# Counting edges with one-hots: eight of a kind in one comparison, item innermost

## What is computed

```python
x = _layernorm(x + layer(x, edge_index), axis=-1)
```

```python
agg = jax.ops.segment_sum(x[src], dst, num_segments=n)   # = counts @ x
```

## Time and profile before

| | us |
|---|---|
| median of three runs | 3100.99 |
| lowest, highest | 3099.07, 3108.09 |
| profiled execution | 3096.49 |
| its span | 3094.6 |
| counting stage within it, about | 128 to 562 |

### The profile page before, as it was taken

One profiled execution on the slowest core, in us unless ns is written; L12 is line 12 of the kernel. 1 busy time (PEld: TensorE's weight loads), 2 busy tenths in 40 slices (PEclk: granted clock), 3 DMA queues, 4 the chain that ended last, 5 costly groups with the idle time before them and its releaser, 6 DMA issues. The chain is left out here.

```text
span 3094.6 us, 39006 instructions
## 1 busy us (share of the span) xinstructions
PE 1888.4 (61%) x7042; PEld 1007.8 (33%) x7043; DVE 2296.7 (74%) x4650; ACT 1832.1 (59%) x2352; POOL 1044.7 (34%) x984
## 2 busy tenths in 40 slices
PE   3354555359798567548846666666666666650636
PEld 1122222223333222112233434343433344430636
DVE  4799999479999678768926777777777777775444
ACT  0166666338888444358927877777777777860010
POOL 1000000000000011013207777777777777753000
PEclk8689898555656699869957777777777777765868
DMA  2144444104544499425614555555555555551616
GB/s 84 41 148 147 147 143 143 59 32 164 185 172 177 196 364 373 191 90 209 231 30 146 168 165 166 162 171 166 166 156 170 164 167 161 166 147 29 265 56 223
DMA packets 288619, 490.59 MB, mean 159 GB/s; under 512 B 39166, under 2 KB 237646, under 8 KB 275718
## 3 DMA queue, kind: packets, MB, share of 16 engines
q1 hardware_dynamic: 254694, 394.56, 36.7%
q0 software_dynamic: 26688, 54.65, 7.4%
q10 hardware_dynamic: 7200, 40.96, 3.4%
HBM read 282.58 MB, written 209.91 MB: 159 GB/s over the span
## 5 line engine op out<-in xcount | busy, mean ns | idle before, releaser
L1794 POOL DMA_INDIRECT es_got<-w,es_idx x808 | 882.3, 1092 | 346.1 <-issue 342.4
L1929 PE MATMUL en_pv<-en_sq,avg 128*128 128x512 f32 x202 | 197.7, 1079 | 371.6 <-ACT en_sq L2036 371.6
L1391 PE MATMUL acc<-src_hot,dst_hot 128*128 128x401 f16 x1008 | 231.6, 382 | 186.7 <-DVE src_hot L1366 166.7
L1366 DVE TENSOR_SCALAR src_hot<-iota,col_key 128x400 f16<-128x400 f16 x1008 | 315.9, 313 | 0.0
L1364 DVE TENSOR_SCALAR dst_hot<-iota_blk,row_key 128x128 f16<-128x128 f16 x1008 | 247.4, 245 | 11.9 <-PE acc L1391 11.4
L803 PE MATMUL pd_dn<-hT,pd_lhs 66*128 66x512 f32 (+1 forms) x350 | 233.3, 845 | 23.0 <-DVE pd_top L906 18.2
L2064 ACT COPY es_rows<-es_rp 128x512 f32<-128x512 f32 x202 | 118.2, 585 | 171.7 <-PE es_rp L1911 170.4
L1992 DVE TENSOR_TENSOR es_lg<-es_dn,es_w2p 128x512 f32<-128x512 f32 x101 | 69.5, 688 | 198.1 <-PE es_w2p L1885 198.1
L1391 PEld LDWEIGHTS acc<-src_hot,dst_hot 128*128 128x128 f16 x1008 | 107.2, 106 | 311.4 <-issue 270.8
L1059 PE MATMUL ns_acc<-ns_w,ns_val 128*65 128x512 f32 (+1 forms) x350 | 156.2, 595 | 71.2 <-DVE ns_w L1019 71.2
L1420 ACT COPY cbuf<-acc 128x401 f32<-128x401 f32 x200 | 98.4, 492 | 146.7 <-PE acc L1391 112.8
(11 more groups left out here) (500 smaller groups left out, 4753.9 us busy)
## 6 DMA issues: line engine op xcount, KB each, us to landing
rows<-es_rows SPq DMA_DIRECT2D x202, 256.0 KB, 2.8
counts_part<-cbuf SPq DMA_DIRECT2D x50, 800.0 KB, 3.7
near<-pd_out SPq DMA_DIRECT2D x25, 1600.0 KB, 6.2
ns_near<-near SPq DMA_DIRECT2D x25, 1600.0 KB, 9.8
ns_cnt<-counts_part SPq DMA_DIRECT2D x25, 1600.0 KB, 6.7
ss_cnt<-counts_part SPq DMA_DIRECT2D x25, 1600.0 KB, 6.6
n_ct<-turned ACTq DMA_DIRECT2D x50, 800.0 KB, 6.0
top_plane<-es_mx SPq DMA_DIRECT2D x101, 256.0 KB
```

The source lines that it names most:

```text
L1366: TS(src_hot[:, s, i, 0:PART].unsqueeze(1), k["iota16"][:, 0:PART].unsqueeze(1), k["col_key"][:, bass.ds(BATCH * b + i, 1)], None, ALU.is_ ...
L1391: last = nc.tensor.matmul(flat[:, bass.ds(places[i], PART + 1)], dst_hot[:, s, i, :], src_hot[:, s, i, 0:PART + 1], start=False, stop=Fals ...
L1794: pool.indirect_dma_start(got[:, s, t, half * 2 * F:(half + 1) * 2 * F], None, d["w23"], bass.IndirectOffsetOnAxis(ap=idx[:, s, half, t:t ...
L1929: nc.tensor.matmul(pv[:, :], avg[:, :], sq[:, :], start=True, stop=True).then_inc(var, 1)
```

## The change

The eight one-hots of a batch are made by one `tensor_tensor` each: one for the eight destinations, one for the eight sources. In the rings the item becomes the innermost dimension, so that an item's one-hot has a step of eight elements. The increasing numbers stand eight times over in two new tiles, `rows_each` and `cols_each`, which two copies fill at the start of the stage. The eight keys of a batch are read again for every row. `row_key` and `col_key` are written in float16, not float32. TensorE takes item i with a step of eight elements for the stationary and for the moving operand, and waits once a batch for both one-hots.

```diff
-        src_hot = sb("src_hot", [P, RING, BATCH, PART + 2], F16)
-        dst_hot = sb("dst_hot", [P, RING, BATCH, P], F16)
+        src_hot = sb("src_hot", [P, RING, PART + 2, BATCH], F16)
+        dst_hot = sb("dst_hot", [P, RING, P, BATCH], F16)
+        rows_each = sb("rows_each_item", [P, P, BATCH], F16)
+        cols_each = sb("cols_each_item", [P, PART, BATCH], F16)
...
+                V.tensor_copy(rows_each[:, :, :], k["iota_blk"][:, :].unsqueeze(2).to_broadcast([P, P, BATCH]))\
+                 .then_inc(each_made, 1)
+                V.tensor_copy(cols_each[:, :, :], k["iota16"][:, 0:PART].unsqueeze(2).to_broadcast([P, PART, BATCH]))\
+                 .then_inc(each_made, 1)
+                dve.wait_ge(each_made, 2)
...
-                        for i in range(BATCH):
-                            TS(dst_hot[:, s, i, :].unsqueeze(1), k["iota_blk"][:, :].unsqueeze(1),
-                               k["row_key"][:, bass.ds(BATCH * b + i, 1)], None, ALU.is_equal)
-                            TS(src_hot[:, s, i, 0:PART].unsqueeze(1), k["iota16"][:, 0:PART].unsqueeze(1),
-                               k["col_key"][:, bass.ds(BATCH * b + i, 1)], None, ALU.is_equal).then_inc(hot, 1)
+                        items = bass.ds(BATCH * b, BATCH)
+                        V.tensor_tensor(dst_hot[:, s, :, :], rows_each[:, :, :],
+                                        k["row_key"][:, items].unsqueeze(1).to_broadcast([P, P, BATCH]), ALU.is_equal)
+                        V.tensor_tensor(src_hot[:, s, 0:PART, :], cols_each[:, :, :],
+                                        k["col_key"][:, items].unsqueeze(1).to_broadcast([P, PART, BATCH]),
+                                        ALU.is_equal).then_inc(hot, 1)
...
+                        pe.wait_ge(hot, b + 1)
                         for i in range(BATCH):
-                            if i % 4 == 0:
-                                pe.wait_ge(hot, BATCH * b + i + 4)
-                            last = nc.tensor.matmul(flat[:, bass.ds(places[i], PART + 1)], dst_hot[:, s, i, :],
-                                                    src_hot[:, s, i, 0:PART + 1],
+                            last = nc.tensor.matmul(flat[:, bass.ds(places[i], PART + 1)], dst_hot[:, s, :, i],
+                                                    src_hot[:, s, 0:PART + 1, i],
...
-            keep(build, ("row_key", [P, NITEM], F32), ("col_key", [P, NITEM], F32), ("places", [1, NITEM], I32),
+            keep(build, ("row_key", [P, NITEM], F16), ("col_key", [P, NITEM], F16), ("places", [1, NITEM], I32),
```

More of the change, by code:

```diff
@@ L1343, in counts @@
         nil_made = sem("nil_made")
+        each_made = sem("each_item_made")
         hot, used, sel_made, deg_got, deg_summed, cleared, passed = (
@@ L1353, in _ @@
             def _(dve):
-                V, TS = nc.vector, nc.vector.tensor_scalar
+                V = nc.vector
                 V.memset(nil[:, :], 0.0).then_inc(nil_made, 1)
                 V.memset(none[:, :], 0.0).then_inc(nil_made, 1)
-                V.memset(src_hot[:, :, :, PART:PART + 2], 1.0).then_inc(used, RING)
+                V.memset(src_hot[:, :, PART:PART + 2, :], 1.0).then_inc(used, RING)
+                V.tensor_copy(rows_each[:, :, :], k["iota_blk"][:, :].unsqueeze(2).to_broadcast([P, P, BATCH]))\
[3 more added lines that the diff above has]
+                dve.wait_ge(each_made, 2)
                 dve.wait_ge(used, RING)
```

## The result

| | before | changed |
|---|---|---|
| median of runs, us | 3103.02 (3099.07 to 3108.09, 4 runs, the three from before the change among them) | 3396.68 (3394.24 to 3397.77, 4 runs) |
| ratio | 1 | 1.0957, 95% interval 1.0931 to 1.0983 |
| span of the profiled execution, us | 3094.6 | 3394.7 |
| mean granted clock of TensorE | 0.755 | 0.687 |

The change makes the kernel 9.6% slower. The forecast of 3091.2 us and its range of 3083 to 3106 both missed. What came is the second rival, whose price was 3360 us.

What follows compares the result with a forecast made beforehand. The prediction took a chain of register reads on TensorE's sequencer to bound the counting stage. Its terms, -1.9 - 11.6 + 1.1 + 1.5 + 1.1, summed to -9.8 us: 3091.2 us as a median, range 3083 to 3106.

Steps and rivals of the forecast that it cites:

- the second rival: Counting stage: spaced reads cost TensorE more, 0.67 us a matmul, +259 us, 3360 us; chance 0.11.
- The chain on TensorE's sequencer: Counting stage: register reads queue behind each batch's matmuls and set the step, 2.66 us undisturbed, 3.00 behind the loop's branch.
- the reads that stretch after a store: TensorE's register reads in the counting stage: lengthened by stores of counts, about 1.3 us each; the change adds +1.1 us.
- the VectorE wait that was not real: Counting stage: 166.7 us of TensorE's waiting is booked on source one-hots, though the comparisons were already over.
- The third rival: Counting stage: TensorE's waits for VectorE are real, so all VectorE's gain counts; -70 us, 3031 us; chance 0.04.
- VectorE's gain: Counting stage: two comparisons a batch take 2.5 us, gaining only in the first batches, where VectorE was truly waited for; -1.9 us.
- The first rival: Counting stage: VectorE gets no second element a cycle, 4.7 us a batch; +177 us, 3278 us; chance 0.05.
- The sequencer's instruction: TensorE's sequencer, counting stage: the second wait's register instruction goes, 0.09 us for each of 126 batches; -11.6 us.
- The start: Head of the counting stage: two copies before the first comparison delay the first batch; +1.5 us, between +0.5 and +5.
- The spaced read: TensorE's operands at a 16-byte step: matmuls 0.334 us apart, showing only in the last batch; +1.1 us.
- The sum without that term: Counting stage: all forecast terms except the +1.1 us for TensorE's reads with a 16-byte step; -10.9 us.
- the fourth rival: Counting stage: right mechanism, but stores fall worse or GpSimd holds up the start; -3 to +3 us, 3098 to 3104; chance 0.05.

Runs made afterwards that it cites:

- the one wait: Kernel before with TensorE waiting once a batch for its one-hots in place of twice, nothing else changed; 3090.58 us, ratio 0.9966.
- the doubled stores: Kernel before with each float32 store of counts made twice, the second time to another place in memory; 3141.47 us, ratio 1.0135.
- the packed kernel: Changed kernel, but TensorE reads both operands from neighbouring elements, without a step, so its counts are wrong; 3083.48 us, ratio 0.9947.
- grouped versions: Changed kernel with items in two groups of four (step 8 bytes), 3085.58 us, or four groups of two (4 bytes), 3087.38 us.

## Why the prediction was wrong

**What bounds the kernel: right.** The chain on TensorE's sequencer, the reads that stretch after a store and the VectorE wait that was not real are borne out by the one wait (-11 us from a single register instruction a batch) and by the doubled stores. The third rival, real waits for VectorE, is out: the packed kernel has all of VectorE's gain and became 18 us faster, not 70.

**VectorE: right, to the hundredth.** It was to take 0.69 + 1.82 us a batch, and took 0.70 and 1.82 in the mean. The Trainium skill ("Vector Engine (DVE) Microarchitecture Reference", section 5.1) states two elements a cycle for two-source instructions on 2-byte operands, a reread row included. The trace agrees: 3200 elements in 1825 ns, where 1600 wider ones took 1824. The first rival, 4.7 us a batch, is out.

**The sequencer's instruction: right.** Forecast -11.6 us, measured -10.8 in the medians and -11 in the steps.

**The start: forecast too high, by a microsecond.** The copies took 0.63 and 1.81 us as forecast, and the first matmul came 5.96 us after the stage's first instruction (131.79) where it had been 5.54. That is +0.4 against the +1.5 taken, just under the lower bound of +0.5. (That the stage begins 3.7 us later lies before it.) The timeline of VectorE at the head of the stage of the changed kernel:

```profile
132.47 0.63 DVE L1361 COPY rows_each_item<-iota_blk 128x1024 f16<-128x1024 f16 x1
133.03 1.81 DVE L1363 COPY cols_each_item<-iota 128x3200 f16<-128x3200 f16 x1
135.19 0.69 DVE L1372 TENSOR_TENSOR dst_hot<-rows_each_item,row_key 128x1024 f16<-128x1024 f16 x1 [0.35 <-DVE cols_each_item L1363]
135.80 1.82 DVE L1374 TENSOR_TENSOR src_hot<-cols_each_item,col_key 128x3200 f16<-128x3200 f16 x1
```

**The spaced read: the step that failed.** A spaced read was put at 0.334 us a matmul, between bounds of 0.173 and 0.67, and took 0.71: even the upper bound was a little low, and the choice between them was wrong. I took 0.334, "the nearest row in which a column takes twice as long", but nothing tied a spaced column to the half clock: it was a number that happened to exist. The trace of the kernel before had no row of the operation, so the whole bracket was open, and the threshold of 0.40 us lay in its lower half. A term of that kind called for a chance nearer to even, not for 0.11, and for a range that reached 3360. The two arguments against the rival both fell. "Still a sixth of slack" presumed the 0.334. "The clock rises with work" is contradicted by the row of 200 to 400 us: the engine was busy without a pause, and the clock stayed at 0.50. What was said for the rival, that both operands are spaced and disturb each other, was not the reason either: the moving operand alone makes the loss. The Trainium skill ("Advanced Engine Details and Errata", section SBUF Cachelines), which wants at least two hits on a 16-byte line and speaks of a penalty otherwise, had the right sign. With 16 bytes the trace agrees: 0.710 us apart in place of 0.173. But two hits are not enough here: two elements lie in such a line at a step of 8 bytes, where the matmuls are 0.357 us apart.

**The sum without that term.** -10.9 us was forecast; the packed kernel became faster by 17.9 in the medians (11 to 22 by its interval). The steps make up 12.0 of it (125 times 3.319 less 3.223). The remaining 6 us stay open. The runs of the kernel before differ among themselves by 18 us in this group (3089 to 3107). In the profiled executions the part after the last matmul of the counting, which the change does not touch, differs by 9.8 us (2544.7 before, 2534.9 packed), so the medians need not owe all of their difference to the change. The range was written down with a slip: the forecast's and the fourth rival's bounds are -16 and +3, and only with the 2 us at either end do they give 3083 to 3106.

**The fourth rival** (stores falling worse, start held up) did not show in the packed version: its reads are 68 us over their undisturbed length where they were 65, near the +1.1 us taken for it, and all packed and grouped versions with the two reads apart came out faster than the kernel before.

## What to carry to other kernels

A layout that makes one engine's writing fast is read by another engine, and both prices are wanted before it is chosen: put the items innermost only as far as the reader's step allows, here two float16 (4 bytes) for TensorE's moving operand. Where the trace has no row for an operation that every iteration would use, and the stage's slack lies between the bounds, measure that operation by itself first, or give the bad end a real chance. And where two chains run at nearly the same pace, try both gains together: the steps of the stage gave 13.5 and 18.7 us alone and 47.7 together.

## What the runs showed that was not expected

- A spaced moving operand costs a time that grows with the bytes it spans and not with the granted clock: 401 columns with a step of 16 bytes in 0.69 us at 1.00 and in 0.71 at 0.50. A step of 4 bytes costs 0.007 us a matmul at the full clock.
- The granted clock stayed at 0.50 for the 700 us of the stage while TensorE was busy without a pause, and so (between 200 and 400 us) in the other three kernels in which half or all of the matmuls had a step of 12 or 16 bytes. It was 0.93 to 0.95 with a step of 8.
- A read of nine registers from SBUF takes 2.17 us at the median from an address that is not a multiple of 16 bytes, and 0.85 from one that is.
- GpSimd's copy of four elements (L1467) takes 1295 ns in the changed kernel and 1002 to 1296 in all others with two two-input comparisons a batch, where it takes 258 to 300 with the sixteen one-input ones. It is off the path in the changed kernel (GpSimd waits 654.5 us for ScalarE before these copies), and no run asked for the cause.
